# Order of work on TensorE in an attention loop: transposes of q and k ahead of the product with V

## What is computed

```
q, k, v = h @ q_w.T + q_b, h @ k_w.T + k_b, h @ v_w.T + v_b      # 16 heads of 128
beta    = softplus(h @ b_w.T + b_b)
attn    = norm(q) @ norm(k).T  in chunks of 64 positions, no softmax
out     = (attn * mask) @ (beta * v)        # mask: causal decay, as the reference has it
out     = (out * silu(h @ og_w.T)) @ o_w.T + o_b
x       = x + ga * out
```

## Time and profile before

| | us |
|---|---|
| three runs | 2203.3, 2204.36, 2204.71; median 2204.36 |
| the profiled execution | 2207.08 |
| its span, first to last instruction | 2205.3 |
| TensorE matmul busy in the span | 2168.8 (98%) |
| VectorE (DVE), ScalarE (ACT), GpSimd (POOL) busy | 1176.3, 1029.9, 537.3 |

### The profile page before, as it was taken

One profiled execution on the slowest core, in us unless ns is written; L12 is line 12 of the kernel. 1 busy time (PEld: TensorE's weight loads), 2 busy tenths in 40 slices (PEclk: granted clock), 3 DMA queues, 4 the chain that ended last, 5 costly groups with the idle time before them and its releaser, 6 DMA issues.

```text
span 2205.3 us, 34017 instructions
## 1 busy us (share of the span) xinstructions
PE 2168.8 (98%) x11420; PEld 1839.8 (83%) x11420; DVE 1176.3 (53%) x2171; ACT 1029.9 (47%) x3284; POOL 537.3 (24%) x540
## 2 busy tenths in 40 slices
PE   7999999999999999999999999999999999999999
PEld 6888888888888888888888887888888888888887
DVE  4455566555556555555555454555555555545554
ACT  4555555555555655556555453333333333333332
POOL 2333334344334334434434442000000000000000
PEclk8999999999999999999999999999999999999999
DMA  7464451453553543542333130343334233323221
GB/s 234 168 195 160 163 163 46 153 154 92 154 144 84 172 152 92 147 147 87 127 118 98 53 134 1 139 173 110 120 106 157 97 120 133 120 101 114 92 101 63
DMA packets 191884, 274.66 MB, mean 125 GB/s; under 512 B 99184, under 2 KB 132960, under 8 KB 191712
## 3 DMA queue, kind: packets, MB, share of 16 engines
q1 hardware_dynamic: 191712, 272.49, 38.8%
HBM read 214.79 MB, written 57.67 MB: 124 GB/s over the span
## 4 chain that ended last, share of the span: by engine, by line
PE 91%; DVE 3%; ACT 2%; issue 2%; DMA 1%; SPq 0%; DVEq 0%; ACTq 0%
PE proj_ps L641 47%; PE out_ps L641 14%; PE av_ps L849 5%; PE s_ps L838 4%; PE s_ps L894 3%; PE av_ps L894 3%; PE kt_ps L894 3%; PE qt_ps L894 3%; PE qt_ps L822 2%; PE kt_ps L827 2%; DMA head_scr<-stage 1%; PE misc_ps L669 1%; ACT squares L1062 1%; PE misc_ps L660 0%; PE out_ps L707 0%
## 5 line engine op out<-in xcount | busy, mean ns | idle before, releaser
L641 PE MATMUL proj_ps<-w_qkv,h_t 128*128 128x512 f32 x2304 | 612.3, 404 | 15.1 <-DVE q_sb L1353 6.8
L641 PEld LDWEIGHTS proj_ps<-w_qkv,h_t 128*128 128x128 f32 x2304 | 409.9, 189 | 97.2 <-issue 14.3
L641 PE MATMUL proj_ps<-h_t,w_qkv 128*128 128x512 f32 x1800 | 443.7, 391 | 0.0
L641 PEld LDWEIGHTS proj_ps<-h_t,w_qkv 128*128 128x128 f32 x1800 | 335.9, 188 | 68.9
L598 POOL TENSOR_TENSOR inv_norm<-guarded,minus_half 128x8 f32<-128x8 f32 x128 | 209.6, 1638 | 662.6 <-DVE guarded L1366 662.5
L1053 ACT ACTIVATE q_t<-qt_ps 128x512 f32<-128x512 f32 x128 | 76.3, 596 | 320.6 <-PE qt_ps L822 320.5
L641 PE MATMUL proj_ps<-h_t,w_gate 128*128 128x512 f32 x768 | 186.9, 398 | 0.5 <-PE misc_ps L695 0.3
L1353 DVE TENSOR_TENSOR q_sb<-proj_ps,bias 128x512 f32<-128x512 f32 x128 | 88.0, 687 | 181.0 <-PE proj_ps L641 174.2
L1062 ACT ACTIVATE squares<-q_sb 128x128 f32<-128x128 f32 x512 | 151.5, 298 | 69.2 <-DVE q_sb L1353 65.3
L641 PEld LDWEIGHTS proj_ps<-h_t,w_gate 128*128 128x128 f32 x768 | 142.7, 190 | 32.4 <-ACT gate L1076 2.5
L1353 DVE TENSOR_TENSOR v_sb<-proj_ps,bias 128x512 f32<-128x512 f32 x128 | 88.5, 691 | 138.7 <-PE av_ps L849 138.2
(11 more groups left out here) (202 smaller groups left out, 3292.6 us busy)
## 6 DMA issues: line engine op xcount, KB each, us to landing
w_qkv<-tile_scr SPq DMA_DIRECT2D x100, 768.0 KB, 4.3
w_qkv<-head_scr SPq DMA_DIRECT2D x45, 1024.0 KB, 11.4
head_scr<-stage SPq DMA_DIRECT2D x30, 512.0 KB, 3.1
w_gate<-head_scr SPq DMA_DIRECT2D x15, 1024.0 KB, 4.9
w_out<-head_scr SPq DMA_DIRECT2D x15, 1024.0 KB, 5.3
tile_scr<-stage SPq DMA_DIRECT2D x25, 512.0 KB, 3.2
x_in<-_attn_hidden_states_dram SPq DMA_DIRECT2D x16, 512.0 KB, 7.3
h_scr<-stage SPq DMA_DIRECT2D x16, 512.0 KB, 3.3
```

Source lines behind the costliest of these rows:

```text
L641: mm = pe.matmul(out, w, y, start=(j == 0 and m == 0), stop=(3 * j + m == n - 1))
```

## The change

In the loop of TensorE `turn(n)` moves from behind `attend(n-1)` to ahead of it. Its waits and its eight transposes move with it. No other engine's list is changed, nothing is added or removed, and no DMA is issued in either.

```diff
                 if t == 2 and i:
                     project_out(i - 1, 1)
+                if 1 <= n <= N:
+                    turn(n)
                 if n >= 2:
                     attend(n - 1)
-                if 1 <= n <= N:
-                    turn(n)
                 if n < 2:
                     for h in range(KC):
                         boot_chunk((G, O)[n], h)
```

## The result

The changed kernel takes 2225.48 us (median of 6 runs, 2225.17 to 2226.35) against 2204.53 before (6 runs, 2203.3 to 2207.02). The ratio is 1.0094, 95% interval 1.0083 to 1.0105: 20.9 us slower. The forecast was slower, 2214.5 with a range of 2207 to 2221. The sign was right. The forecast growth, 10.2 us, was half of what was measured, and 2225.48 lies outside the range. The profiled execution took 2225.17 us.

The account below looks back on a forecast made before the run. TensorE, busy 98% of the span, was taken as the bound, so only gaps between matmuls count. Losses of 15.2 us less a gain of 5.0 gave +10.2 on the median 2204.36: 2214.5 us, range 2207 to 2221.

Parts of the forecast that it names:

- The gain of 5.0 us: Product with V behind the masked scores: 18 waits, all shorter than 0.87 us, covered; 5.0 us (bounds 0 and 8.1).
- Item 1: Gate iterations (t == 1): V's later bias delays the third gate product, 0.14 us in 23 of 31, 3.2 us.
- Item 2: At t == 2 the second output sum ends later, delaying side-task transposes in `out_ps`: 0.31 us, 14 iterations, 4.3 us.
- Item 3, statistics: Layernorm statistics on DVE behind V's bias make Q's bias late: six iterations, up to 0.58 us each, 2.2 us.
- Item 3, `split`: Five `split` iterations: the shifted first low part no longer waits for POOL; only two pay 0.16 each, 0.3 us.
- Item 3, start of the loop: Two iterations at the start of the loop, with long DVE side tasks behind V's bias, pay 0.80 and 0.35 us.
- Item 4, `log`: Where ACT is full behind the gated output, as with `log` table loads, K comes later: six iterations, 1.96 us.
- Item 5: One turn, now starting earlier, waits for its scaled q: 0.15 us.
- rival C: The 0.14 margin is missing: K waits 0.1 to 0.15 us in about 60 iterations; 2222 us, chance 0.08.
- rival D: The turns often wait for POOL's scaled q, 0.9 us or more; 2223 us with 10 cases, chance 0.03.
- the last of my signs of being wrong: On TensorE, a different distance between records at the new seams, which would change the length without any wait.
- Rival A: Product with V: all 18 score waits go, with new waits below 5.0 us; faster, 2201 us, chance 0.07.

Follow-up runs that it names:

- run 4: Changed kernel with a third buffer for v, so V's bias waits for the product with V of two iterations ago: 2201.96 us, ratio to before 0.9984.
- run 5: Kernel before, with only the transposes of q ahead of the product with V, in every iteration: 2206.87 us against 2205.73, ratio 1.0009.
- run 7: Kernel before, with only the transposes of q ahead, in the 14 iterations whose product with V had waited for scores: 2202.28 us, ratio 0.9986.
- run 3: Changed kernel with the output's second sum ahead of the bias of V on DVE at t == 2: 2217.34 us, ratio to before 1.005.
- run 2: Kernel before, with the turns ahead of the product with V only below iteration 15: 2211.64 us, ratio 1.003.
- run 8: Kernel before, with both turns ahead only in gate iterations (t == 1) from n >= 15: 2205.8 us against 2205.73, ratio 1.0002.
- run 1: Kernel before, with the turns ahead of the product with V only in iterations 15 and later: 2219.38 us against 2205.75, ratio 1.006.
- run 9: Kernel before, in its old order, with a third buffer for v: 2199.18 us against 2204.89, ratio 0.9977.

## Why the prediction was right in sign and wrong in size

**What bounds the kernel, and the path of the loss: right.** TensorE's gaps decide; the bias of V is the edge that hands the lateness on. Runs 4 and 5 show it.

**The gain of 5.0 us: right in place, and near in size.** The waits for scores went from 18 to 3; run 7 got 3.4 us back alone.

**Item 1, gate iterations, 0.14 each: right.** In the changed kernel an iteration whose bias is not late otherwise:

```profile
605.42 0.69 DVE L1353 TENSOR_TENSOR v_sb<-proj_ps,bias 128x512 f32<-128x512 f32 x1 [0.77 <-PE av_ps L849]
...
605.07 5.90 PE L641 MATMUL proj_ps<-h_t,w_gate 128*128 128x512 f32 x24
```

5.90 against 5.73, 0.17 where I had 0.14, and 31 waits for ACT where there were 6.

**Item 2, the second sum: right in place, number and size.** 14 waits (L707 and L686), 0.51 us each at the loader; by the starts of the products the iterations with them lost 0.27 to 0.32, and I had said 0.31. All iterations with t == 2 from 14 on grew by 4.25 us together, against 4.3. What I missed is that the sum also stands in front of the gated output, so that DVE and ACT stayed late behind it: run 3 won 2.4 us in the iterations that follow.

**Item 3, statistics: right.** The iteration of the earlier trace rows after the change:

```profile
1141.74 0.60 PE L822 MATMUL qt_ps<-ident,q_sb 128*128 128x128 f32 x4
...
1147.65 1.66 PE L641 MATMUL proj_ps<-w_qkv,h_t 128*128 128x512 f32 x6 [0.33 <-DVE q_sb L1353]
...
1143.78 0.69 DVE L1353 TENSOR_TENSOR v_sb<-proj_ps,bias 128x512 f32<-128x512 f32 x1 [1.51 <-PE av_ps L849]
...
1146.83 0.17 DVE L1158 TENSOR_SCALAR var_eps<-mean_var 128x4 f32<-128x4 f32 x1
1146.91 0.69 DVE L1353 TENSOR_TENSOR q_sb<-proj_ps,bias 128x512 f32<-128x512 f32 x1
```

The bias of V starts 2.04 after TensorE's group began (forecast 2.03). var_eps takes 0.17 in place of 0.46, and Q's bias comes 5.17 after the group's start where it came 4.59 after: the shift of 0.58 is as worked out. The Trainium skill ("SBUF — State Buffer", section "SBUF: two separate sides") says that VectorE and GpSimd share a pair of ports, which whichever starts first holds to its end, when the VectorE instruction runs in a two-port mode, or has two SBUF inputs and the GpSimd one reads SBUF. Both rows fit that; which mode var_eps runs in, no row shows.

**Item 3, `split`: wrong.** I let the first low part go free of POOL, because DVE moves by 0.87 and POOL stays. POOL moved as well:

```profile
263.07 1.89 DVE L1175 TENSOR_TENSOR h_t<-h_f,h_t 128x512 fp32r<-128x512 f32 x2 [1.74 <-ACT h_t L985]
...
262.77 1.04 POOL L610 TENSOR_TENSOR v_sb<-v_sb,v_scale 128x512 f32<-128x512 f32 x1
...
266.12 1.66 PE L641 MATMUL proj_ps<-w_qkv,h_t 128*128 128x512 f32 x6 [0.29 <-DVE q_sb L1353]
```

The pair still takes 1.89 (2.09 in the earlier trace rows) beside POOL's scaling of v, which now starts at 4.77 after the group began and not at 4.10, since ACT's squares and so `guarded` were late themselves. Forecast for this V product, of iteration 21: 0.16 at most. Measured: it starts 1.35 us after the q.k product (264.77), where 0.81 is plain, 0.54 late. In iteration 25 that distance grew from 1.37 to 2.06. Iterations 21, 25 and 89 stand behind a `split`; they grew by 0.46 to 0.49 each although a wait for scores of some 0.4 went away in each. Less the 0.17 of the gate, that is about 0.7 each, 2.1 us where the term for all five had 0.3.

**Item 3, start of the loop: the step that failed most.** I counted 0.80 and 0.35 there and set four covered waits for scores against them: about nothing. Run 2 measured 5.9. The waits were in the right place, and one was 0.5 too small: from the q.k product to V, iteration 4 grew by 0.78 us (1.14 to 1.92) and iteration 5 by 0.87 (2.56 to 3.43). What the sum lacks altogether is the clock. The prediction says that the same instruction follows the same one at the same distance over the whole loop; at the start it does not, and the lower clock behind the longer wait cost 1.65 us in one profile and some 3 of the 5.9 by the estimate above. The delay was not carried whole through the start: the gaps of iterations 6 and 7 are as before, and the wait at 186.21 is ACT's for a DMA. What is left of the 5.9, 1 to 2 us, is open. Single iterations from 8 to 13, which wait for DMAs, differ by up to 2.6 us between profiles that have the old order there (iteration 12 in run 8 and before).

**Item 4, `log`: right for the case shown.** V's bias there starts at 340.19 and K at 340.93 with 0.86 of idle TensorE:

```profile
340.93 1.67 PE L641 MATMUL proj_ps<-w_qkv,h_t 128*128 128x512 f32 x6 [0.86 <-DVE v_sb L1353]
```

**Item 5 and rivals C, D: no turn waits for POOL's q in number, and K of plain iterations does not wait.** Plain iterations in the loop's tail have grown by 0.01 to 0.02 us each, over 125 iterations at most 2 us, which I had at 0. They have grown as much in runs 1, 3 and 4, and not at all in runs 2 and 9, whose order is the old one there: it belongs to the order on TensorE, the last of my signs of being wrong.

The sum: between iterations 14 and 127 my terms give about 10 (15.2 less the 1.15 at the start and 0.6 of early gate and `prep` iterations, less the 3.3 of gain that falls there), measured 13.5. The `split` term (about 1.8 us short), the plain iterations (1 to 2) and the gates (0.17 for 0.14, some 0.6) account for the gap. At the start: about 0, measured 5.9. The chances I gave to "slower" add up to 0.79 and not to 0.81; nothing hangs on it. Rival A, the faster one, failed where the text said: the new waits were above 5.0 us. That the waits can be covered without new ones is true only of less work ahead (run 7) or of an edge cut elsewhere (run 4).

## What to carry to other kernels

When a group of instructions moves ahead of another on a full engine, the one that is pushed back needs the closer look: list who waits for its end and what stands behind that waiting instruction on its engine, because a helper with no idle time behind it hands the delay on whole (0.85 of 0.87 us in iteration 5). Ask also what a longer wait does to the clock of the full engine, and look at the granted clock of each stretch before an excess is put down to waits. Put ahead only as much as the wait is long, and where a buffer's release is the edge, one more buffer takes the edge away for whichever order (0.9977 alone, 0.9967 with four transposes ahead in 14 iterations).

## What the runs showed that I had not expected

Half the shift (0.44 us) cost about 1 us and the whole (0.87) cost 20.9: the margins of the gate iterations and of the second sum lie between them, while plain iterations have room for both. A third buffer that no row of the kernel before points to as a wait of TensorE brought 5.7 us, since DVE's idle time for the product with V (138.2 us in the earlier trace rows) was harmless in most iterations; what the buffer gained from iteration 14 on was 3.9 us, and 3.4 of it fell on the gate iterations, t == 1. The same wait of 2.37 us was followed by the lower clock in three profiles and not in a fourth. And a delay on ACT can move POOL's work so that it keeps meeting the same DVE instruction, so a collision may not go away when both are moved.
